# Local attention blocks: GpSimd's half of the keys ahead of the normalising products, VectorE's second rotary product ahead of the row sums

## What is computed

```python
def attn_layer(x, Wqkv, qs, ksc, Wo):
    q, k, v = jnp.split(x @ Wqkv, 3, -1)               # 16 heads of 64
    q = l2norm(q) * qs
    k = l2norm(k) * ksc
    q = q * cos * scale + rotate_half(q) * sin * scale
    k = k * cos / scale + rotate_half(k) * sin / scale
    out = local_attention(q, k, v)                     # windows of 32: own keys and the window's before
    return out @ Wo
...
    sim = jnp.einsum('bhwie,bhwje->bhwij', bq, bk2) * 8.0
    sim = jnp.where(mask, -finfo.max, sim)
    attn = jax.nn.softmax(sim, -1)
    out = jnp.einsum('bhwij,bhwje->bhwie', attn, bv2)
...
for i in range(6):
    x = attn_layer(shift_tokens(x), ...) + x
    x = ffn_layer(shift_tokens(x), ...) + x
```

## Time and profile before

| | |
|---|---|
| median of 3 runs | 3153.22 us (3150.84 to 3154.32) |
| profiled execution, its own time | 3146.83 us |
| its span, first to last instruction | 3144.8 us |
| TensorE's mean granted clock | 0.954 of full speed |

### The profile page before, as it was taken

One profiled execution on the slowest core, in us unless ns is written; L12 is line 12 of the kernel. 1 busy time (PEld: TensorE's weight loads), 2 busy tenths in 40 slices (PEclk: granted clock), 3 DMA queues, 4 the chain that ended last, 5 costly groups with the idle time before them and its releaser, 6 DMA issues. The chain is left out here.

```text
span 3144.8 us, 72108 instructions
## 1 busy us (share of the span) xinstructions
PE 2774.6 (88%) x27244; PEld 1692.0 (54%) x27244; DVE 2442.2 (78%) x3071; ACT 2104.3 (67%) x3079; POOL 1351.6 (43%) x1209
## 2 busy tenths in 40 slices
PE   5799999997678989888889898989999999789997
PEld 3122222223546565656566666656665656478885
DVE  3899999992379797979798888888888979455554
ACT  2488888885158787878788787878787878311111
POOL 1000000000078685867586758676766767200000
PEclk7799999998589999999999999999999999889998
DMA  3011111100010001000100010001000000000001
GB/s 131 27 29 28 28 29 29 29 24 8 8 57 9 6 9 43 7 8 9 42 9 6 17 34 9 8 15 36 8 7 14 15 7 9 12 18 0 0 0 34
DMA packets 56465, 64.35 MB, mean 20 GB/s; under 512 B 24742, under 2 KB 38964, under 8 KB 55348
## 3 DMA queue, kind: packets, MB, share of 16 engines
q1 hardware_dynamic: 55380, 60.58, 7.0%
q10 hardware_dynamic: 864, 0.79, 0.1%
HBM read 36.69 MB, written 7.34 MB: 14 GB/s over the span
## 5 line engine op out<-in xcount | busy, mean ns | idle before, releaser
L886 DVE TENSOR_REDUCE a_minus_max<-a_ps_max 128x1 f32<-128x1024 f32 x512 | 596.8, 1218 | 57.6 <-PE a_ps_max L811 52.3
L794 ACT ACTIVATE a_expT<-a_ps_scoresT 128x512 f32<-128x512 f32 (+1 forms) x683 | 528.8, 808 | 78.2 <-PE a_ps_scoresT L829 67.4
L1178 POOL TENSOR_TENSOR b_turned_q<-b_rot_q,b_turned_q 128x1024 f32<-128x1024 f32 x96 | 226.8, 2362 | 270.2 <-DVE b_turned_q L1549 257.3
L844 PE MATMUL a_ps_out<-a_expT,v_aug 128*32 128x256 f32 x4096 | 327.9, 392 | 5.4 <-ACT a_outT L781 4.8
L1620 DVE STREAM_TRANSPOSE b_probsT<-b_probs 32x512 f32<-32x512 f32 x384 | 269.4, 702 | 11.9 <-POOL b_probs L1219 0.3
L765 POOL CAST a_max_hi<-a_minus_max 128x16 bf16<-128x16 f32 x32 | 6.3, 198 | 631.1 <-DVE a_minus_max L886 631.1
L1287 ACT ACTIVATE b_kT<-b_psD 64x512 f32<-64x512 f32 x384 | 226.1, 589 | 58.6 <-PE b_psD L1374 53.5
L829 PE MATMUL a_ps_scoresT<-a_q_op,a_k_op 26*128 26x512 bf16 x1024 | 247.2, 385 | 13.1 <-ACT a_expT L794 4.4
L1225 POOL TENSOR_TENSOR b_turned_k<-b_rot_k,b_turned_k 128x512 f32<-128x512 f32 x192 | 243.9, 1270 | 0.2 <-DVE b_turned_k L1549 0.2
L1185 POOL TENSOR_TENSOR b_rot_q<-b_turned_q,b_inv_norm 128x1024 f32<-128x1024 f32 x96 | 182.8, 1904 | 137.7 <-issue 137.7
L1219 POOL TENSOR_TENSOR b_probs<-b_probs,b_inv_sum 128x512 f32<-128x512 f32 x192 | 197.3, 1049 | 99.1 <-DVE b_inv_sum L1593 99.1
(11 more groups left out here) (295 smaller groups left out, 6019.4 us busy)
## 6 DMA issues: line engine op xcount, KB each, us to landing
b_v_edge<-b_v SPq DMA_DIRECT2D x96, 128.0 KB
b_w_qkv<-L_ffn_Wqkv SPq DMA_DIRECT2D x6, 1536.0 KB
a_q_op<-terms_q SPq DMA_DIRECT2D x128, 48.0 KB
a_k_op<-terms_k SPq DMA_DIRECT2D x128, 48.0 KB
joined<-a_outT SPq DMA_DIRECT2D x256, 16.0 KB
b_w_o<-L_ffn_Wo SPq DMA_DIRECT2D x6, 512.0 KB
a_q_op<-a_max_rows SPq DMA_DIRECT2D x128, 4.0 KB
b_w<-L_ffn_W SPq DMA_DIRECT2D x6, 341.0 KB
```

Of the source, the lines that this page charges most:

```text
L794: act.activation(expT[:, to:to + 512 * size], ps_scoresT[:, at:at + 512 * size], ACT.Exp, scale=SCALE_A).then_inc(exp_ready, 1)
L844: last_mm = pe.matmul(ps_out[lo:lo + 32, 256 * part:256 * part + 256], v_aug[:, b * T8 + kt, head, :], expT[:, at:at + 256], start=(kt == ...
L886: dve.tensor_reduce(minus_max[p % 2][:, side, 0, qt:qt + 1], ps_max[u % 2][:], AX.X, ALU.max, negate=True).then_inc(max_taken, 1)
L1178: pool.tensor_tensor(turned[:], rot[:], turned[:], ALU.add).then_inc(added, 1)
```

## The change

On GpSimd, the two halves of the keys are no longer done together after the two normalising products. The first half's sum and product come first, then the two normalising products, then the second half's sum and product. On VectorE, the sine product of the keys comes right after the cosine product, ahead of the row sums and their inverse. On TensorE, the mask's two matmuls stand between the turns of the first and of the second half of the keys. No instruction is added or removed.

```diff
@@ -1212,23 +1212,32 @@
                     add(rot_q, turned_q, parts_q_ready, sum_q_ready)
                     tokens_of((b * T8 + s + 1) % TILES, 1 - par)
                     unit(rot_q, turned_q, sum_q_ready, unit_q_ready, qT_half, 0)
+                def unit_keys(half):
+                    heads = slice(8 * half, 8 * half + 8)
+                    pool.wait_ge(parts_k_ready, 2 * T + 2)
+                    pool.tensor_tensor(turned_k[:, heads], rot_k[:, heads], turned_k[:, heads], ALU.add).then_inc(sum_k_ready, 1)
+                    pool.wait_ge(sum_k_ready, 2 * T + half + 1)
+                    pool.wait_ge(inv_norm_ready, T + 1)
+                    pool.wait_ge(kT_half, 2 * T)
+                    pool.tensor_tensor(rot_k[:, heads], turned_k[:, heads],
+                                       inv_norm[:, HEADS_B + 8 * half:HEADS_B + 8 * half + 8].unsqueeze(2).to_broadcast([P, 8, DH]),
+                                       ALU.mult).then_inc(unit_k_ready, 1)
+                def normalise(c):
+                    pool.wait_ge(inv_sum_ready, T)
+                    pool.tensor_tensor(probs[:, :, c, :], probs[:, :, c, :],
+                                       inv_sum[:].unsqueeze(2).to_broadcast([P, HEADS_B, W]), ALU.mult).then_inc(probs_ready, 1)
+                if 0 in lags:
+                    unit_keys(0)
                 if 1 in lags:
-                    pool.wait_ge(inv_sum_ready, T)
-                    for c in range(2):
-                        pool.tensor_tensor(probs[:, :, c, :], probs[:, :, c, :],
-                                           inv_sum[:].unsqueeze(2).to_broadcast([P, HEADS_B, W]), ALU.mult).then_inc(probs_ready, 1)
+                    normalise(0)
+                if 1 in lags:
+                    normalise(1)
                 if 0 in lags:
-                    pool.wait_ge(parts_k_ready, 2 * T + 2)
-                    for half in range(2):
-                        heads = slice(8 * half, 8 * half + 8)
-                        pool.tensor_tensor(turned_k[:, heads], rot_k[:, heads], turned_k[:, heads], ALU.add).then_inc(sum_k_ready, 1)
-                        pool.wait_ge(sum_k_ready, 2 * T + half + 1)
-                        pool.wait_ge(inv_norm_ready, T + 1)
-                        pool.wait_ge(kT_half, 2 * T)
-                        pool.tensor_tensor(rot_k[:, heads], turned_k[:, heads],
-                                           inv_norm[:, HEADS_B + 8 * half:HEADS_B + 8 * half + 8].unsqueeze(2).to_broadcast([P, 8, DH]),
-                                           ALU.mult).then_inc(unit_k_ready, 1)
+                    unit_keys(1)
 
             tokens_of(0, 0)
             tables(0)
@@ -1364,9 +1373,9 @@
                     pe.wait_ge(w_qkv_in, 16 * (l + 1))
                 w_at = l % 2 * 3 * INNER
 
-                def turn(src, unit, parts, held, done):
-                    for half in range(2):
+                def turn(src, unit, parts, held, done, halves=(0, 1)):
+                    for half in halves:
                         pe.wait_ge(unit, parts * (T - 1) + half % parts + 1)
                         if held is not None:
                             pe.wait_ge(held, 2 * (T - 1) + half + 1)
@@ -1396,14 +1405,14 @@
                         pe.wait_ge(y_ready, GROUPS * l + 2 * b - (2 if isinstance(s, int) else 0))
                     project(psK, k_ready, parts_k_ready, square_k_ready, INNER)
                 if 1 in lags:
-                    turn(rot_k, unit_k_ready, 2, qT_held, kT_half)
-                if 1 in lags:
+                    turn(rot_k, unit_k_ready, 2, qT_held, kT_half, (0,))
 
                     if 2 in lags:
                         pe.wait_ge(z_ready, T - 2)
                     for half in range(2):
                         pe.matmul(psS[:, 512 * half:512 * half + 512].rearrange("p (a b) -> p a b", b=2 * W), ident_b[:],
                                   band[:, ds(tile_at(b, s, 1), 1), :].to_broadcast([P, 8, 2 * W]), start=True, stop=False, skip_group_check=True)
+                    turn(rot_k, unit_k_ready, 2, qT_held, kT_half, (1,))
                     pe.wait_ge(qT_held, 2 * T)
                     pe.wait_ge(kT_old, T)
                     for half in range(2):
@@ -1583,6 +1592,8 @@
                 if ahead:
                     dve.wait_ge(w_mlp_in, 16 * 13 * (ahead[0] + 1))
                     centre(ahead[0], ahead[1], 0)
+                if 0 in lags:
+                    rotary_sin(psK, turned_k, parts_k_ready, 2)
                 if 1 in lags:
 
                     dve.wait_ge(exp_ready, T)
@@ -1591,8 +1602,6 @@
                     if 2 in lags:
                         dve.wait_ge(probs_ready, 2 * (T - 1))
                     dve.reciprocal(inv_sum[:], row_sum[:]).then_inc(inv_sum_ready, 1)
-                if 0 in lags:
-                    rotary_sin(psK, turned_k, parts_k_ready, 2)
                 def add_projection():
 
                     dve.wait_ge(wo_ready, T - 1)
```

## The result

The changed kernel takes 3289.76 us (median of 3 runs, 3287.62 to 3296.79) against 3153.22 before: a ratio of 1.044, 95% interval 1.0413 to 1.0466, which is 136.5 us between the medians. The forecast of 3297 us is 7 us above it, and the time lies inside the range of 3275 to 3325.

A forecast was written before the change was run, and what follows sets the result against it. VectorE was taken to set the pace. 84 x 1.64 = 137.8 us plus 11 x 0.55 = 6.1 us, together 143.9 us, gave 3290.7 us on the profiled execution and 3297 us as median; range 3275 to 3325.

The forecast's parts named there:

- The term of 1.64 us: Loop steps without `ahead`: `packed` starts at 13.44 instead of 11.80, behind GpSimd's first normalising product; 1.64 us in 84 steps.
- The 0.1 us allowed for a wait instruction: On GpSimd, between the keys' product and the normalising product: a wait instruction might cost some 0.1 us.
- The steps with `ahead`: 11 steps where VectorE already waits for TensorE's projection: `packed` 0.14 us later, the MLP's start 0.55 us; 6.1 us together.
- The wait did not stay hidden: Rejected claim at `packed`: GpSimd's first product ready when inverse sums end; only 20.9 us of exponential waits go, 3132 us; 0.03.
- Only the normalising product uncovered: At `packed`: the keys' half done by then, `packed` 0.98 us later in 84 steps; 82 us, 3235 us; chance 0.04.
- GpSimd was not held off by VectorE's reads: Rejected claim: GpSimd's sum held until VectorE's row sums end, 1.2 us more in 95 steps; 114 us, 3411 us; 0.03.
- No second wait grew: Rejected claim: exponential or scores arrive late as TensorE's and ScalarE's orders shift; 84 us more, 3381 us; chance 0.04.
- TensorE's waits for keys shrank as foreseen: Sign in the profile after: TensorE's waits for keys shrink at the turns and return elsewhere.
- rival 1: At `packed`: GpSimd's first product ready by the inverse sums' end; only 20.9 us of exponential waits go, 3132 us; chance 0.03.

## Why the prediction was right

**What sets the pace.** VectorE, as read from the earlier trace rows. The mask's move alone shows it from the other side: it takes from TensorE's largest wait and gives nothing to the time.

**The term of 1.64 us.** In offsets from the step's start, forecast and measured: sine product 8.74 and 8.71, row sums 9.96 and 9.84, end of the inverse sums 11.56 and 11.42, GpSimd's sum 10.01 and 10.00, normalising product 12.36 and 12.36, `packed` 13.44 and 13.44, the next step 17.59 and 17.59. The idle time was put at 1.88 us and is 2.02, because the row sums started 0.12 us earlier than thought (sine product to row sums is 1.13 us, not 1.22); that does not move `packed`, which hangs on GpSimd's chain. The 0.1 us allowed for a wait instruction did not show (1.01 us from the keys' product to the normalising product, forecast 1.00). Nor is it one step alone: 66 of the 95 distances from one `packed` to the next are 1.61 to 1.66 us longer than before. VectorE's move alone is 0.81 us of the term, for the uncovered normalising product; GpSimd's move on top of it, as in the run with both, adds the other 0.83, for the half of the keys ahead of that product. The single moves do not add up: GpSimd's alone costs 3.11 us in a step.

**The steps with `ahead`.** In the timeline of VectorE they answer to the earlier trace rows:

```profile
1713.79 0.68 DVE L1531 TENSOR_TENSOR b_centred<-z,b_psS 128x512 f32<-128x512 f32 x1
...
1719.11 0.71 DVE L1623 STREAM_TRANSPOSE b_packed<-b_probs 128x512 f32<-128x512 f32 x1
1720.11 0.70 DVE L1629 STREAM_TRANSPOSE b_probsT<-b_probs 32x512 f32<-32x512 f32 x1 [0.29 <-POOL b_probs L1230]
1720.84 0.75 DVE L1543 SCALAR_TENSOR_TENSOR b_scaled<-b_centred,b_vecs,b_psS 128x512 f32<-128x512 f32 x1
```

From `centred`, `packed` comes 0.17 us later than before (5.32 against 5.15) and `scaled` 0.57 us later (7.05 against 6.48); the forecast said 0.14 and 0.55.

**The sum.** 143.9 us forecast; 140.8 us in the stage of the two profiled executions and 2 us in the step ahead of it; 136.5 us between the medians, whose interval of the ratio is 130 to 147 us. What the sum left out is small and goes both ways: the row maximum waits 8.0 us (13 waits) instead of 12.6 (16), and slower matmuls in the MLP cost some 5 us (below). That these two nearly cancel is luck; the 1.64 us a step are not.

**The rivals.** The wait did not stay hidden: it is 171.8 us. Only the normalising product uncovered is what VectorE's move alone shows (1.16 us idle), not the full change. GpSimd was not held off by VectorE's reads: its sum starts at 1627.21 inside the row sums (1627.05 to 1628.26) and takes the usual 1.27 us. The lock of the Trainium skill, page "SBUF — State Buffer", section "Who interferes with whom", leaves out reductions, and this trace agrees. No second wait grew in the loop's steps: row maximum and row sums wait less than before. Outside of them VectorE's wait at `centred` in the MLP went from 34.6 to 41.6 us (11 waits each), behind the slower matmuls. TensorE's waits for keys shrank as foreseen (its weight loads' from 200.3 to 90.0 us) and came back at the scores, for ScalarE's key copies (104.5 us), without making the row maximum wait longer.

**What was not foreseen.** That one of the moves without the others would draw on TensorE's clock (27 us), as the section on it shows. In the full change the four matmuls of that section are slow in 9 halves of 12, before in 6 of 12: 3 more at some 1.7 us each, 5 us that lie within the 140.8. The prediction had also taken the 0.21 us ahead of the row sums as a gain that rival 1 would bring; the exponential moved on its own shows that the wait can come back at the row maximum.

## What to carry to other kernels

Before an instruction is moved on the engine that sets the pace, look at what another engine does meanwhile for the next instruction in its queue: the moved one may be the cover, and what it covered is then paid in full. The chain from the last operand over the helper's queue to the waiting instruction could be added up here from single rows to a few hundredths of a microsecond, with the hand-overs in it. A long wait of an engine that does not set the pace was worth nothing, however high it stood in the list, and filling a wait helped only until the next product that the same queue waits for.

## What the runs showed of the hardware

The same four matmuls of 512 columns behind the same waits (0.89 us, 1.16 us of work, 1.69 us) ran in 1.95 us in some halves and in about 3.6 us in others, within one execution: in the kernel before in 6 halves each (3.38 to 3.75 us in the slower), with VectorE's move alone slower in 9 of 12, with the mask's move added in 1 of 12. The granted clock of 4 us around them is 0.60 in a slow half (levels of 1.2 and 2.4 GHz mixed) and 1.00 in a quick one. So a change that leaves these matmuls alone can move the time by some 1.7 us for each such place, through the clock, and no row read here tells in which direction.
